# Three layers in one kernel: the latent layer's weights are loaded and folded earlier, and the expert layer's set-up moves into its main block

## The chip, the cores and the metric

The kernel runs on one core of one Trainium2 chip. TensorE (PE) multiplies matrices, VectorE (DVE), ScalarE (ACT) and GpSimd (POOL) do elementwise work, SyncE (SP) issues most DMAs. The metric is the device time of one execution in microseconds (us), as the median of several runs; lower is better.

## The reference

`x` has 8 batches of 512 tokens with 256 channels, in f32. Six steps follow each other, each on a layernorm of x:

```
x = x + 0.5 * L0_ffn(layernorm(x))     # 8 experts, gate's top 1; all experts are summed
x = x + L0_attn(layernorm(x))          # attention among the 16 heads of a token
x = x + 0.5 * L0_ffn(layernorm(x))
x = x + 0.5 * L1_ffn(layernorm(x))     # routed: 63 chosen tokens of a batch
x = x + L1_attn(layernorm(x))          # latent attention
x = x + 0.5 * L1_ffn(layernorm(x))
```

The routed layer weighs each token with one column, takes the best 63 of each batch, runs rope attention with an attention mask, gathered by row, and a gelu MLP over them, and puts them back. `position_ids` gives the angle of each token. The latent layer has 16 heads of 64, and a latent of 64:

```
q = x @ Wq;  c = x @ Wkv_down;  k = c @ Wk_up;  v = c @ Wv_up
out = softmax(causal(q @ k.T / 8)) @ v;  x = x + out @ Wout
```

## The kernel before, in words

`macaron_kernel` builds four layers one after the other: `expert_and_head_layers` (the first three steps), `routed_layer`, `latent_attention_layer`, `routed_layer` again. x stays in SBUF throughout. Each layer is a row of blocks.
**Expert layer.** A set-up block (L295 to L360) issues the load of batch 0 and of four weight chunks on SP, nine small loads on POOL, transposes three of the small tensors on TensorE and copies them on VectorE. In the main block SP loads the other weight chunks into four slots of `stage`; ScalarE writes their f16 high half (`split_chunk_head`), VectorE the low half (`split_chunk_tail`). Sixteen stages of 32 hidden tiles follow, each `up` and `down` in three f16 products, gelu on ScalarE, the low half of gelu on POOL (L760). The attention among heads runs on VectorE between them (`head_piece`). In the last stage VectorE does the router's statistics of seven batches ahead (`RouterEarly`).

**Routed layer.** The opening block (L1003 to L1119) loads the weights and the position rows (SP), makes index tiles (POOL), normalises x into `y` (32 operations on ScalarE, L1117) and picks the tokens: VectorE does the statistics of the last batch, waits for TensorE's transposes of `w_col` (L1099), then finds the best 64 in eight rounds (L1061, L1063), marks and numbers them (to L1088); TensorE transposes the marks (L1105). VectorE's list begins with a wait on the position rows' DMA and their cast (L1033). The main block starts with `one_hot` (L1508) and does attention and MLP.

**Latent layer.** The opening block (L1723 to L1827) loads the five weights, turns `Wk_up`, `Wv_up` and `Wq` on TensorE, and multiplies them head by head to `a` (Wq times Wk_up) and `b` (Wv_up times Wout): for each of 8 pairs of heads TensorE writes banks of PSUM (L1772, L1775), ScalarE writes the f16 high halves (L1825, L1826) and VectorE the low halves (L1813, L1815). POOL makes constants (L1735 to L1746), VectorE casts them and sets parts of the key, value and query tiles (L1782 to L1793). The main block is a pipeline over batches and heads (`stream`); its first operations are the layernorm statistics of batch 0 on VectorE, the variance on POOL, and the first guess of the root on VectorE (L49).

## Time and profile before

| | us |
|---|---|
| median of 3 runs | 2885.16 |
| lowest and highest run | 2885.03, 2890.66 |
| the profiled execution | 2883.19 |
| its span, first to last instruction | 2881.4 |

Busy time in that span: PE 2485.0 (86%), DVE 2123.2 (74%), ACT 1570.0 (54%), POOL 844.4 (29%). The page cuts the span in 40 slices of 72 us; a digit is the busy share in tenths, PEclk the granted clock of TensorE in tenths of 2.4 GHz:

```profile
PE   6999999989999999999999567688988888898376
PEclk9999999999999999999999666599999999999677
```

The expert layer fills the first 22 slices, the first routed layer is around slices 23 and 24, the latent layer follows to slice 37, and the second routed layer ends the row.

### The profile page before, as it was taken

The numbers are of one execution on the slowest core, as the hardware profiler recorded it, in microseconds if no ns is written. First come the engines' busy times: TensorE is split into PE (matmuls) and PEld (weight loads), VectorE is DVE, ScalarE is ACT, GpSimd is POOL, SyncE is SP. The second block draws the span as 40 slices with busy tenths as digits, with TensorE's granted clock in tenths as the row PEclk, the third lists the DMA queues.
The fourth block names the chain that finished last, engine by engine and source line by source line (L and its number), as shares of the span: only waits on it lengthen the run. The fifth ranks groups of instructions, "written<-read, shape, count | busy, mean of one in ns | idle before, by whom it ended". The sixth has DMA issues, their size and how long they took to land. (4 is left out here: it accounts for less than half of the span.)

```text
span 2881.4 us, 39763 instructions
## 1 busy us (share of the span) xinstructions
PE 2485.0 (86%) x14369; PEld 1352.2 (47%) x14369; DVE 2123.2 (74%) x3942; ACT 1570.0 (54%) x2517; POOL 844.4 (29%) x816
## 2 busy tenths in 40 slices
PE   6999999989999999999999567688988888898376
PEld 3444444444444444444444355255655555565254
DVE  3479688878979886888715654489788879877754
ACT  5655454555555554545554341277667767767251
POOL 3444333434443443434444100002112112202200
PEclk9999999999999999999999666599999999999677
DMA  5000000000000000000000101000000000000101
GB/s 167 28 1 1 0 1 1 1 1 1 1 1 1 1 1 1 1 1 1 1 1 1 63 1 38 1 1 2 2 2 3 2 3 2 2 2 2 49 16 59
DMA packets 29189, 33.11 MB, mean 11 GB/s; under 512 B 6408, under 2 KB 25416, under 8 KB 28984
## 3 DMA queue, kind: packets, MB, share of 16 engines
q1 hardware_dynamic: 28008, 27.89, 3.1%
q0 software_dynamic: 976, 2.56, 0.3%
q8 instruction: 120, 1.97, 0.3%
q14 instruction: 85, 0.70, 0.1%
HBM read 25.59 MB, written 4.19 MB: 10 GB/s over the span
## 5 line engine op out<-in xcount | busy, mean ns | idle before, releaser
L760 POOL TENSOR_TENSOR g_lo<-g_full,g_hi 128x512 f16<-128x512 f32 x512 | 659.0, 1290 | 910.1 <-ACT g_hi L851 908.1
L851 ACT ACTIVATE g_full<-hid,b_col 128x512 f32<-128x512 f32 x512 | 351.7, 687 | 559.5 <-PE hid L152 558.1
L150 PE MATMUL hid<-y_hi,w_hi 128*128 128x512 f16 x1024 | 396.0, 387 | 37.6 <-DVE y_lo L837 34.9
L151 PE MATMUL hid<-y_lo,w_hi 128*128 128x512 f16 x1024 | 395.2, 386 | 0.0
L152 PE MATMUL hid<-y_hi,w_lo 128*128 128x512 f16 x1024 | 394.7, 385 | 0.0
L150 PE MATMUL acc<-g_hi,w_hi 128*128 128x512 f16 x1024 | 388.9, 380 | 0.0
L151 PE MATMUL acc<-g_lo,w_hi 128*128 128x512 f16 x1024 | 388.9, 380 | 0.0
L152 PE MATMUL acc<-g_hi,w_lo 128*128 128x512 f16 x1024 | 388.6, 379 | 0.0
L851 ACT ACTIVATE g_hi<-hid,b_col 128x512 f16<-128x512 f32 x512 | 349.0, 682 | 0.0
L2095 DVE TENSOR_REDUCE mla_m_col<-mla_ps 128x1 f32<-128x512 f32 (+3 forms) x512 | 225.0, 483 | 62.3 <-PE mla_ps L1937 56.5
L2220 ACT ACTIVATE mla_p_full<-mla_ps 128x1280 f32<-128x1280 f32 x128 | 158.4, 1237 | 139.5 <-PE mla_ps L1967 139.2
L2195 DVE TENSOR_TENSOR mla_p_lo<-mla_p_full,mla_p_hi 128x1280 f16<-128x1280 f32 x128 | 205.5, 1605 | 3.2 <-ACT mla_p_hi L2220 2.6
L2257 POOL TENSOR_TENSOR mla_o_lo<-mla_o,mla_o_hi 128x512 f16<-128x512 f32 x64 | 107.2, 1680 | 326.6 <-ACT mla_o_hi L2229 326.6
L1936 PE MATMUL mla_ps<-mla_key_hl,mla_q_hi 128*128 128x512 f16 (+3 forms) x512 | 130.5, 308 | 69.3 <-DVE mla_m_col L2095 68.6
L721 DVE TENSOR_TENSOR prod<-score,v_rows 128x1024 f32<-128x1024 f32 x128 | 178.5, 1394 | 3.0
L150 PEld LDWEIGHTS hid<-y_hi,w_hi 128*128 128x128 f16 x1024 | 101.4, 99 | 161.7 <-DVE y_lo L837 38.9
L684 DVE TENSOR_TENSOR prod<-qk_rot 128x1024 f32<-128x1024 f32 x128 | 173.2, 1353 | 3.3
L1963 PE MATMUL mla_ps<-mla_q_hi,mla_key_hl 128*128 128x512 f16 (+3 forms) x512 | 156.3, 305 | 8.9 <-issue 6.4
L152 PEld LDWEIGHTS hid<-y_hi,w_lo 128*128 128x128 f16 x1024 | 101.8, 99 | 125.7 <-issue 8.6
L687 DVE TENSOR_REDUCE score<-prod 128x64 f32<-128x1024 f32 x128 | 156.2, 1220 | 4.4
L723 DVE TENSOR_REDUCE o_rows<-prod 128x64 f32<-128x1024 f32 x128 | 156.2, 1220 | 4.4
L2220 ACT ACTIVATE mla_p_hi<-mla_ps 128x1280 f16<-128x1280 f32 x128 | 157.6, 1231 | 0.0
(370 smaller groups left out, 4837.7 us busy)
## 6 DMA issues: line engine op xcount, KB each, us to landing
stage<-in_L_ffn_w_dram SPq DMA_DIRECT2D x16, 512.0 KB, 4.9
x<-in_L_attn_x_dram SPq DMA_DIRECT2D x8, 512.0 KB, 8.1
routed_w<-in_L_ffn_w_dram SPq DMA_DIRECT2D x4, 1024.0 KB, 8.1
out_dram<-x SPq DMA_DIRECT2D x8, 512.0 KB, 4.5
mla_sums<-mla_sum_row SPq DMA_DIRECT2D x128, 2.0 KB
mla_wq<-in_L_attn_Wq_dram SPq DMA_DIRECT2D x1, 1024.0 KB, 7.0
mla_wout<-in_L_attn_Wout_dram SPq DMA_DIRECT2D x1, 1024.0 KB, 9.2
routed_wqkv<-in_L_ffn_wq_dram SPq DMA_DIRECT2D x2, 256.0 KB, 2.9
```

The costliest lines, as they stand in the source:

```text
L150: pe.matmul(out, w_hi, v_hi, start=first, stop=False)
L151: pe.matmul(out, w_hi, v_lo, start=False, stop=False)
L152: return pe.matmul(out, w_lo, v_hi, start=False, stop=final)
L684: dve.tensor_tensor(pr, q4, k4, ALU.mult).then_inc(head_step, 1)
L687: dve.tensor_reduce(score[:, row:row + GROUP, :], pr, AX.X, ALU.add).then_inc(head_step, 1)
L721: dve.tensor_tensor(pr, e4, v4, ALU.mult).then_inc(head_step, 1)
L760: pool.tensor_tensor(g_lo[:, g, :], g_full[:, g, :], g_hi[:, g, :], ALU.subtract).then_inc(tail_done, 1)
L851: act.activation(out[:, g, :], hid[:, ht % 4, :], ACT.Gelu, bias=b1_col[:, ht:ht + 1], scale=1.0 / WS).then_inc(gelu_done, 1)
L1963: pe.matmul(flat[:, at:at + cols], key_hl[:, (slot + (h + 1) // H) % 2, toks], q_hi[:, hh % RING, t * P:], start=True, stop=False)
L2095: dve.tensor_reduce(m_col[:, g % 2, t, j:j + 1], flat[:, QUERY_AT[t]:QUERY_AT[t] + (t + 1) * P], AX.X, ALU.max).then_inc(s_max, 1)
L2195: dve.tensor_tensor(p_lo[:, hh % 2, :], p_full[:, hh % 2, :], p_hi[:, hh % 2, :], ALU.subtract).then_inc(p_tail, 1)
L2220: act.activation(out[:, hh % 2, :], flat[:, 3 * 512:3 * 512 + KEY_COLS], ACT.Exp, scale=float(MLA_DIM) ** -0.5).then_inc(exp_done, 1)
```

## The change

- The expert layer's set-up block is gone. Its loads, transposes (`small_turns`, into a bank of `acc`) and copies (`small_copies`) stand in the main block; TensorE and ScalarE wait for the five copies (`small_out`) before the first stage.
- `LatentSources`: `stage` becomes a tile that lasts into the first routed layer. Behind the last weight chunk SP waits for all chunk tails and loads the latent weights into it and into two smaller tiles.
- The position rows are loaded in the expert layer, cast once in its last stage and kept in `RouterEarly` for both routed layers.
- `LatentFold`: turns, folds and splits stand in the first routed layer's opening block. ScalarE copies from PSUM to f32 tiles, POOL makes both f16 halves. Six of the eight pairs stand on TensorE ahead of the pick's transposes, two behind. ScalarE's copies alternate with its normalisation from batch 2 on. POOL makes and casts the constants too. The second routed layer has no fold.
- The latent layer has no opening block. `set_tiles` holds the memsets, behind the statistics of batch 0; TensorE and SP wait for them.
- Tiles of the routed main block share memory (`sq` with `rot`, `p_t` with `mask_rows`, `o` and `o_t` with `mask_t`, `proc` with `s`), and its softmax waits for the last rotation.

```diff
+    def load(self, sp):
+        io = self.io
+        sp.dma_start(self.wk[:, :], io["Wk_up"].rearrange("c h n -> c (h n)")).then_inc(self.k_in, 16)
+        sp.dma_start(self.wv[:, :], io["Wv_up"].rearrange("c h n -> c (h n)")).then_inc(self.v_in, 16)
+        sp.dma_start(self.wq[:, :, :], io["Wq"].rearrange("(k p) h n -> p k (h n)", p=P)).then_inc(self.q_in, 16)
+        sp.dma_start(self.wout[:, :, :], io["Wout"].rearrange("(m h) n d -> (h n) m d", h=2)).then_inc(self.out_in, 16)
+        sp.dma_start(self.down[:, :, :], io["Wkv_down"].rearrange("(k p) c -> p k c", p=P)).then_inc(self.down_in, 16)
...
+        def small_turns(pe):
+            pe.wait_ge(small_in, 16 * SMALL_LOADS)
+            pe.wait_ge(ones_set, 1)
...
+            last.then_inc(small_t, 1)
+        def small_copies(dve):
+            dve.wait_ge(small_t, 1)
+            dve.tensor_copy(b1_col[:, :], small[:, 0:HID_TILES]).then_inc(small_out, 1)
...
+            dve.tensor_tensor(gate_lo[:, :, :], gate_t[:, :, :], gate_hi[:, :, :], ALU.subtract).then_inc(small_out, 1)
+        SMALL_STEPS = 5
...
+                small_turns(pe)
                 pe.wait_ge(normed, TILES)
                 transpose_tiles(pe, y, turn, ident[:, :]).then_inc(y_turned, 1)
+                pe.wait_ge(small_out, SMALL_STEPS)
...
+                small_copies(dve)
...
+                sp.dma_start(x[:, 0], io["x"][0].rearrange("(t p) d -> p t d", p=P)).then_inc(x_first, 16)
+                for c in range(SLOTS):
+                    load_chunk(sp, c)
...
+                sp.dma_start(early.pos_rows[:, :], io["position_ids"][:, 0:SEQ].rearrange("b (t p) -> b t p", p=P)
+                             ).then_inc(router_in, 16)
+                sp.wait_ge(chunk_tail, len(chunks))
+                sources.load(sp)
             @block.gpsimd
             def _(pool):
+                small_loads(pool)
...
+                act.wait_ge(small_out, SMALL_STEPS)
...
+    def turn(self, pe):
+        ps, first = self.ps, self.FIRST_BANK
+        for i, (w, there) in enumerate(((self.wk, self.k_in), (self.wv, self.v_in))):
+            pe.wait_ge(there, 16)
+            for m in range(MLA_PAIRS):
+                last = pe.transpose(ps[:, first + i, m * LATENT:(m + 1) * LATENT], w[:, m * P:(m + 1) * P],
+                                    self.ident[i * LATENT:(i + 1) * LATENT, i * LATENT:(i + 1) * LATENT])
+            last.then_inc(self.turned, 1)
+        pe.wait_ge(self.q_in, 16)
+        for m in range(MLA_PAIRS):
+            if m == 6:
+                pe.wait_ge(self.turn_out, 1)
+            bank = first + (2, 3, 4, 0)[m // 2]
+            for k in range(KD):
+                at = (m % 2) * D + k * P
+                last = pe.transpose(ps[:, bank, at:at + P], self.wq[:, k, m * P:(m + 1) * P], self.ident[:, :])
+            if m % 2 == 1:
+                last.then_inc(self.turned, 1)
+    def fold(self, pe, m):
+        if m == 0:
+            pe.wait_ge(self.out_in, 16)
+            pe.wait_ge(self.turn_out, 6)
+        if m >= 2:
+            pe.wait_ge(self.fold_out, m - 1)
+        for i in range(2):
+            bank = self.bank(m, i)
+            rows = slice(i * MLA_DIM, (i + 1) * MLA_DIM)
+            for k in range(KD):
+                pe.matmul(self.ps[:, bank, k * LATENT:(k + 1) * LATENT], self.wq_t[rows, m, k * P:(k + 1) * P],
+                          self.wk_t[rows, m, :], start=True, stop=True)
+            last = pe.matmul(self.ps[i * LATENT:(i + 1) * LATENT, bank, D:2 * D], self.wv_t[rows, m, :],
+                             self.wout[rows, m, :], start=True, stop=True)
+        last.then_inc(self.folded, 1)
+    def turned_copies(self, act):
...
+    def folded_copies(self, act, m):
+        act.wait_ge(self.folded, m + 1)
+        if m >= 2:
+            act.wait_ge(self.split_step, 4 * (m - 1))
+        for i in range(2):
+            rows = slice(i * LATENT, (i + 1) * LATENT)
+            act.activation(self.b_full[rows, m % 2, :], self.ps[rows, self.bank(m, i), D:2 * D], ACT.Copy, scale=WS)
+            last = act.activation(self.a_full[:, m % 2, :, i, :], self.folded_a(m, i), ACT.Copy, scale=WS)
+        last.then_inc(self.fold_out, 1)
+    def constants(self, pool):
+        to, made = self.to, self.made
...
+        for n, base in enumerate((0, -32)):
+            pool.wait_ge(made, 2 + n)
+            pool.affine_select(out=self.spread_f[:, :, :], in_=self.spread_f[:, :, :], compare_op=ALU.not_equal,
+                               fill=1.0 / INV_SCALE, base=base, pattern=[[-1, MLA_HEADS], [0, LATENT]],
+                               channel_multiplier=1).then_inc(made, 1)
...
+        pool.wait_ge(made, 6)
+        pool.tensor_copy(to.spread[:, :, :], self.spread_f[:, :, :])
+        pool.tensor_copy(to.block_q[:, :], self.block_f[:, 0, :])
+        pool.tensor_copy(to.block_k[:, :], self.block_f[:, 1, :])
+        pool.tensor_copy(to.ident_b[:, :], self.ident[:, :])
+        pool.wait_ge(self.down_in, 16)
+        pool.tensor_scalar(self.down[:, :, :], self.down[:, :, :], WS, None, ALU.mult).then_inc(self.down_step, 1)
+        pool.wait_ge(self.down_step, 1)
+        for i in range(2):
+            pool.tensor_copy(to.down_hi[:, :, i, :], self.down[:, :, :]).then_inc(self.down_step, 1)
+        pool.wait_ge(self.down_step, 3)
+        for i in range(2):
+            pool.tensor_tensor(to.down_lo[:, :, i, :], self.down[:, :, :], to.down_hi[:, :, i, :], ALU.subtract)
+    def split(self, pool, m):
+        to, slot = self.to, m % 2
+        a_hi, a_lo = (w[:, :, 2 * m:2 * m + 2, :] for w in (to.a_hi, to.a_lo))
+        pool.wait_ge(self.fold_out, m + 1)
+        pool.tensor_copy(a_hi, self.a_full[:, slot, :, :, :]).then_inc(self.split_step, 1)
+        pool.tensor_copy(to.b_hi[:, m, :], self.b_full[:, slot, :]).then_inc(self.split_step, 1)
+        pool.wait_ge(self.split_step, 4 * m + 2)
+        pool.tensor_tensor(a_lo, self.a_full[:, slot, :, :, :], a_hi, ALU.subtract).then_inc(self.split_step, 1)
+        pool.tensor_tensor(to.b_lo[:, m, :], self.b_full[:, slot, :], to.b_hi[:, m, :],
+                           ALU.subtract).then_inc(self.split_step, 1)
...
+                    if fold is not None:
+                        fold.constants(pool)
+                        for m in range(MLA_PAIRS):
+                            fold.split(pool, m)
-                    dve.wait_ge(small_in, 16)
-                    dve.tensor_copy(pos_rows_f[:, :], pos_rows[:, :]).then_inc(col_out, 1)
...
-                    pe.wait_ge(col_out, 1)
-                    pe.transpose(ps[:, 1, 0:16], pos_rows_f[:, :], ident[0:16, 0:16]).then_inc(cols_turned, 1)
+                    pe.transpose(ps[:, 1, 0:16], early.pos_rows_f[:, :], ident[0:16, 0:16]).then_inc(cols_turned, 1)
+                    if fold is not None:
+                        fold.turn(pe)
                     pe.wait_ge(weigh_step, TILES + 2)
                     for t in range(TILES):
                         last = pe.transpose(ps[0:BATCH, 0, t * P:(t + 1) * P], w_col[:, :, t], ident[:, :])
                     last.then_inc(rows_turned, 1)
+                    if fold is not None:
+                        for m in range(FOLDS_EARLY):
+                            fold.fold(pe, m)
                     pe.wait_ge(pick_step, 2 + 2 * (ROWS // 8) + 9)
                     for i, r in ((0, 5), (1, 3)):
                         for t in range(TILES):
                             last = pe.transpose(ps[:, 2, at:at + BATCH], row[:, r, t * P:(t + 1) * P],
                                                 ident[0:BATCH, 0:BATCH])
                     last.then_inc(cols_turned, 1)
+                    if fold is not None:
+                        for m in range(FOLDS_EARLY, MLA_PAIRS):
+                            fold.fold(pe, m)
                 @block.scalar
                 def _(act):
+                    if fold is not None:
+                        fold.turned_copies(act)
                     for b in range(BATCH):
                         if b == early.BATCHES:
                             act.wait_ge(norm_step, COLUMNS_AT)
+                        if fold is not None and b >= BATCH - FOLDS_EARLY:
+                            fold.folded_copies(act, b - BATCH + FOLDS_EARLY)
                         for t in range(TILES):
                             col = TILES * b + t
                             act.activation(y[:, b, t, 0:D], x[:, b, t, :], ACT.Identity, bias=shift[:, col:col + 1],
                                            scale=rstd[:, col:col + 1])
+                    if fold is not None:
+                        for m in range(FOLDS_EARLY, MLA_PAIRS):
+                            fold.folded_copies(act, m)
...
+                dve.wait_ge(rot_step, 8 * PAIRS)
...
+        def set_tiles(dve):
+            dve.memset(key_top[LATENT:P, :, :], 0.0).then_inc(zeroed, 1)
+            for slot in range(2):
+                dve.memset(val_hi[:, slot, :, LATENT:P], 1.0)
+                dve.memset(val_lo[:, slot, :, LATENT:P], 0.0)
+            dve.wait_ge(zeroed, 1)
+            dve.memset(key_top[LATENT:LATENT + 1, :, :], M_SCALE)
+            dve.memset(q_lo[LATENT:P, :, :], 0.0)
+            dve.memset(inv_hl[:, :], 0.0).then_inc(zeroed, 1)
...
+                if isinstance(b, int) and after == 0:
+                    set_tiles(dve)
...
+                pe.wait_ge(zeroed, 2)
```

## Rows read from the trace of the kernel before

**Rows 1.** Windows: stretch, length, busy of PE, PEld, DVE, ACT, POOL (count), PEclk, DMA, GB/s.

```profile
110.00:150.00 40.00, 40.00 (x196) 18.89 (x195) 15.29 (x54) 25.45 (x41) 15.89 (x14) 1.00 0.00 1
...
1585.00:1617.00 32.00, 2.32 (x13) 1.46 (x13) 25.34 (x74) 15.83 (x32) 1.88 (x12) 0.50 0.33 108
...
1762.00:1813.00 51.00, 39.22 (x128) 24.39 (x128) 20.23 (x53) 9.56 (x32) 4.17 (x12) 0.50 0.17 54
...
1790.00:1800.00 10.00, 10.00 (x30) 5.66 (x29) 3.33 (x11) 3.33 (x12) 0.00 (x0) 0.50 0.00 0
```

**Rows 2.** Timeline of the start: start us, us, engine, line, op [idle before].

```profile
13.22 0.31 PE L351 MATMUL small<-ident,b_rows 32*128 32x32 f32 x1 [13.22 <-DMA rope<-in_rope_tab_dram]
...
14.60 0.19 DVE L338 COPY b_col<-small 128x32 f32<-128x32 f32 x1 [14.60 <-PE small L358]
...
15.66 1.41 DVE L74 BATCH_NORM_STATS2 stats<-x 128x6 f32<-128x256 f32 x4 [0.30 <-PEq L314]
...
20.25 2.35 DVE L284 SCALAR_TENSOR_TENSOR w_lo<-stage,w_hi 128x1024 f16<-128x1024 f32 x2
...
24.50 1.29 DVE L646 CAST y_hi<-turn 128x512 f16<-128x512 f32 x2 [1.90 <-PE turn L144]
...
27.17 0.61 PE L150 MATMUL hid<-y_hi,w_hi 128*128 128x512 f16 x1 [2.71 <-DVE y_lo L649]
```

**Rows 3.** DMA issues of the first 16 us: KB each, us from issue to landing.

```profile
x<-in_L_attn_x_dram SPq DMA_DIRECT2D x1, 512.0 KB, 4.1
```

**Rows 4.** Timeline of the first routed layer's opening block, up to its main block.

```profile
1585.86 0.81 SPq L1006 DMA_DIRECT2D routed_pos_rows<-_L_ffn_position_ids_dram  x1
...
1588.31 0.21 DVE L1033 CAST routed_pos_rows_f<-routed_pos_rows 16x128 f32<-16x128 int32 x1 [4.86 <-DMA routed_pos_rows<-_L_ffn_position_ids_dram]
...
1595.42 1.02 PE L1099 MATMUL routed_ps<-ident,router_w_col 128*8 128x128 f32 x4 [6.55 <-DVE router_w_col L1043]
...
1615.82 1.02 PE L1105 MATMUL routed_ps<-ident,routed_row 8*128 8x8 f32 x8 [19.38 <-DVE routed_row L1088]
...
1617.42 1.81 POOL L1428 MEMSET routed_v_blk<- 128x2048 f32 x1 [29.66 <-POOLq L1003]
...
1617.46 2.77 DVE L1508 TENSOR_TENSOR routed_one_hot<-routed_iota_row,routed_slot_col 128x256 f32<-128x256 f32 x8 [0.30 <-PEq L1003]
```

**Rows 5.** Timeline of POOL and of DVE late in the expert stage, 1536 us.

```profile
1536.65 1.16 POOL L760 TENSOR_TENSOR g_lo<-g_full,g_hi 128x512 f16<-128x512 f32 x1 [1.43 <-ACT g_hi L851]
...
1536.71 1.13 DVE L57 TENSOR_TENSOR router_newton<-router_rstd 128x28 f32<-128x28 f32 x1
```

**Rows 6.** Timeline of the latent layer's opening block and first steps.

```profile
1762.69 0.26 POOL L1735 MEMSET mla_norm_const<- 128x4 f32 x6 [131.71 <-POOLq L2345]
...
1764.23 2.44 POOL L1740 TENSOR_SCALAR_AFFINE_SELECT mla_spread_f<-mla_spread_f 128x1024 f32<-128x1024 f32 x2
...
1768.29 0.27 DVE L1787 MEMSET mla_val_hi<- 128x256 f16 x1
...
1770.96 3.67 PE L1759 MATMUL mla_ps<-ident,mla_wq 128*128 128x128 f32 x16 [1.28 <-DMA mla_wq<-in_L_attn_Wq_dram]
...
1772.43 0.91 DVE L1793 MEMSET mla_key_top<- 1x1024 f16 x1 [0.27 <-DVE mla_key_top L1791]
...
1781.43 0.38 ACT L1825 ACTIVATE mla_b_hi<-mla_ps 64x256 f16<-64x256 f32 x1 [46.04 <-PE mla_ps L1775]
...
1782.37 0.28 ACT L1826 ACTIVATE mla_a_hi<-mla_ps 128x128 f16<-128x128 f32 x1
...
1813.48 1.41 DVE L74 BATCH_NORM_STATS2 mla_stats<-x 128x6 f32<-128x256 f32 x4 [0.32 <-PEq L1723]
...
1817.08 0.17 DVE L49 TENSOR_SCALAR mla_rstd<-mla_var 128x4 int32<-128x4 int32 x1 [2.20 <-POOL mla_minus_half L124]
```

**Rows 7.** One tile, mla_ps, in 1762:1813: min/median/max ns, first and last start.

```profile
L1775 PE MATMUL mla_ps<-mla_wout,mla_wv_t x32: 631/657/683, 1778.2 to 1809.9; 64*64 64x256 f32 x32
```

**Rows 8.** Timeline of DVE, the second routed layer's opening.

```profile
2700.66 0.21 DVE L1033 CAST routed_pos_rows_f<-routed_pos_rows 16x128 f32<-16x128 int32 x1 [6.02 <-DMA routed_pos_rows<-_L_ffn_position_ids_dram]
```

More of the change, by code:

```diff
@@ L152, in split_matmul, with __init__, sb, sem @@
     return pe.matmul(out, w_lo, v_hi, start=False, stop=final)
+BF16 = mybir.dt.bfloat16
+LATENT = 64
+MLA_HEADS, MLA_DIM = 16, 64
+MLA_PAIRS = MLA_HEADS // 2
+BLOCKED = -1.0e30
+M_SCALE, INV_SCALE = 64.0, 256.0
+GROUP_HEADS = 4
+LEAD = 8
+RING = LEAD
+SUM_SLOTS = 4
+SUM_ROWS = P // MLA_HEADS
+KEY_AT = (0, 512, 1024, 896)
+KEY_COLS = sum(SEQ - t * P for t in range(TILES))
+QUERY_AT = (512 + 384, 0, 512, 0)
+QUERY_TILES = (3, 2, 0, 1)
+PV_BANK = (7, 2)
+class LatentSources:
+    def __init__(self, nc, stack, program, io):
+        def sb(name, shape, dt=F32):
+            return stack.enter_context(nc.sbuf_tensor(f"latent_{name}", shape, dt, side="right"))
+        def sem(name):
+            return program.enter_context(nc.semaphore(f"latent_{name}"))
+        self.stack, self.io = stack, io
+        self.stage = sb("stage", [P, 4, 1024])
+        self.wq = self.stage[:, 0:KD, :]
+        self.wout = self.stage[:, KD:2 * KD, :].rearrange("p a n -> p (a n)").rearrange("p (m d) -> p m d", m=MLA_PAIRS)
+        kv = sb("kv", [P, MLA_HEADS * MLA_DIM])
+        self.wk, self.wv = kv[0:LATENT, :], kv[LATENT:P, :]
+        self.down = sb("down", [P, KD, LATENT])
+        self.k_in, self.v_in, self.q_in = sem("k_in"), sem("v_in"), sem("q_in")
+        self.out_in, self.down_in = sem("out_in"), sem("down_in")
+    def load(self, sp):
[5 more added lines that the diff above has]
+        sp.dma_start(self.down[:, :, :], io["Wkv_down"].rearrange("(k p) c -> p k c", p=P)).then_inc(self.down_in, 16)
 class RouterEarly:
@@ new lines, in small_turns @@
+        def small_turns(pe):
+            pe.wait_ge(small_in, 16 * SMALL_LOADS)
+            pe.wait_ge(ones_set, 1)
+            pe.transpose(small[:, 0:HID_TILES], b1_rows[:, :], ident[0:HID_TILES, 0:HID_TILES])
+            for k in range(KD):
+                pe.matmul(small[:, 64 + k:65 + k], b2_rows[:, k * P:(k + 1) * P], ones[:, :], start=True, stop=True)
+            for k in range(KD):
+                last = pe.transpose(small[:, 128 + k * EXPERTS:128 + (k + 1) * EXPERTS],
+                                    gate_rows[:, k * P:(k + 1) * P], ident[0:EXPERTS, 0:EXPERTS])
+            last.then_inc(small_t, 1)
@@ L944, in routed_layer @@
+def routed_layer(nc, keep, tag, x, ident, early, io, out=None, sources=None, latent=None):
     with ExitStack() as ctx:
@@ L996, in routed_layer @@
             cols_turned = tsem("cols_turned")
+            fold = LatentFold(nc, part, tsem, ps, ident, sources, latent) if latent is not None else None
+            if fold is not None:
+                part.push(sources.stack)
+            FOLDS_EARLY = MLA_PAIRS - 2
             COLUMNS_AT = TILES + LN_COLUMN_STEPS + 1
@@ L1118, in _ @@
                                            scale=rstd[:, col:col + 1])
+                    if fold is not None:
+                        for m in range(FOLDS_EARLY, MLA_PAIRS):
+                            fold.folded_copies(act, m)
         BLOCKS = HEADS // 4
@@ L2349, in _ @@
                             sp.sem_clear(semaphore)
-        layer(expert_and_head_layers, x, ident, early, experts)
-        layer(routed_layer, "routed1", x, ident, early, routed)
-        layer(latent_attention_layer, x, ident, early, latent)
+        with ExitStack() as lasting:
+            sources = LatentSources(nc, ExitStack(), ctx, latent)
+            layer(expert_and_head_layers, x, ident, early, sources, experts)
+            weights = LatentWeights(nc, lasting)
+            layer(routed_layer, "routed1", x, ident, early, routed, None, sources, weights)
+            layer(latent_attention_layer, x, ident, early, weights)
         layer(routed_layer, "routed2", x, ident, early, routed, out)
```

342 lines of the change are left out of this document (109 added, 233 removed).

## The prediction, made before the result was known

> **What bounds the kernel now.** I read the 40 slices of the page first. TensorE is at nine tenths in most slices of the expert stage, and there nothing but its own work counts (the window from 110 to 150 us: 40.00 of 40 us [rows 1]). The change touches none of that steady work, so I looked for the stretches where TensorE is not the bound and the blocks meet at barriers. The windows name two. The first routed layer's opening block (1585 to 1617) has 2.32 us of TensorE in 32 us and 25.34 us of VectorE: a serial chain on VectorE bounds it. The latent layer's opening block (1762 to 1813) has 39.22 us of TensorE at a granted clock of 0.50, the 1.2 GHz level, with no other engine above half: folding the weights on a slow TensorE bounds it. A third is the start, before the first `hid` matmul at 27.17 us [rows 2]. Then I read the timelines of each. Times below are counted from a block's first instruction where I say "at +x".
>
> **The start (set-up moved into the main block).** Before, the small loads land at 13.22, TensorE turns them, VectorE copies them at 14.60, then comes a barrier, and only then does VectorE start the layernorm of batch 0, at 15.66. Its chain runs to 20.25, where the two weight tails begin [rows 2]. The first batch had been there for long: x lands 4.1 us after its issue [rows 3], about 6 us. After the change the layernorm runs at 6 to 10.7 us (20.25 - 15.66 = 4.6 us of chain), under the wait for the small loads. ScalarE's halves of the first two chunks and the four applications also fit before 14.6. What is late next is the small loads: 13.22, TensorE done at 14.60, eight transposes (22.50 to 24.50 before, so 2.0) to 16.6. Beside them VectorE copies (0.8 us) to 15.4, then the tails (2.35) to 17.8, then four halves of y (24.50 to 27.17: 2.67) to 20.5. The first `hid` matmul starts there: 27.17 - 20.5 = **6.7 us gained**. All of it reaches the end, for TensorE is full afterwards. Bounds: 4 (if weight chunks or ScalarE come later than x) to 7.5.
>
> The latent loads (2.6 MB) and the position rows go to SP's queue behind the last chunk; SP has nothing later there, and nobody waits. The added cast of the position rows lies in VectorE's idle time. Both cost nothing.
>
> **Position rows.** The first routed block starts at 1585.86 and VectorE's chain only at 1588.45, after a cast that waited for a DMA [rows 4]. That goes: 2.6 us in each routed layer. In the first it enters the block sum below. In the second [rows 8] nothing else changes, so **2.6 us gained** (0 to 3).
>
> **The latent layer's opening block goes.** It runs from 1762.69 to VectorE's first statistics at 1813.48 [rows 6]: **50.8 us gained**. Given back: the memsets of the key, value and query tiles now stand on VectorE between the statistics and the root's first guess. Before, they ran from 1768.29 to 1773.34 (start of the last plus 0.91), 5.05 us with a 0.5 us gap; I take 4.8. The guess came 3.60 us after the statistics began (1817.08 - 1813.48); now it comes at 1.45 + 4.8 = 6.25: **2.65 us lost** (2.2 to 5, the upper end if VectorE and POOL get in each other's way).
>
> **The first routed layer's opening block grows.** Everything the fold needs is added to it, and it ends when the slowest of four engines ends. Step by step:
>
> - TensorE's 32 turns. Sixteen took 3.67 us [rows 6]; the smaller sixteen take at most as much. They end between +4 and +7.6.
> - VectorE's chain: w_col was ready at 1595.42, or +9.56; less 2.6 that is +7.0. But POOL now works beside it. A POOL subtraction of 1.16 us begins at 1536.65 and a VectorE operation of 28 columns, begun 0.06 us later, lasts 1.13 us, up to the same moment [rows 5]. Eight `one_hot` operations run beside a POOL memset in 2.77 us, 0.35 us each, unhindered [rows 4]. So POOL operations that read SBUF block VectorE's two-input ones. Here POOL reads from about +3.4: two selects of 1.22 us each [rows 6], two smaller, the casts, the split of `down`, about 7 us in all, across VectorE's 16 last small operations. I charge 3.0 us (0, if they slip between, to 5): w_col at +10.0.
> - TensorE turns w_col (1.02 us): +11.05. Then six pair folds. Sixteen half folds spanned 1777.2 to 1810.5, so 2.08 us each, 4.16 us a pair [rows 7]; the last matmul's 0.66 us is added to its start. Six take 25.0: +36.0. ScalarE (four copies, 1.22 us, and one batch of four applications at 15.83/32 = 0.49 us each [rows 1]: 3.2 us a pair) and POOL (below) are both faster than 4.16, so TensorE sets this pace.
> - The pick on VectorE takes 1596.44 to 1615.82, 19.4 us. It would be ready at +30.5, but its eight transposes stand behind the sixth fold in TensorE's order and start at +36.0. They end at +37.0.
> - The last two folds: 8.3 us, +45.35. ScalarE copies the last, 1.25: +46.6. POOL splits it: four operations of 256 columns. Rows 5 have 512 columns in 1.16 us; with the fixed part I take 0.68 for a subtraction and 0.5 for a cast, 2.4 us with the waits: +49.0. The barrier: +49.3.
>
> Before, the main block began at 1617.42, +31.56 [rows 4]. So **17.7 us lost**. ScalarE's applications, 15.83 us alone, end well before this. Bounds: +8 if the fold ran at the fast clock throughout, +22 if POOL is slow and the blocking is full.
>
> **Two rules of the Trainium skill.** "SBUF — State Buffer", section "Who interferes with whom", says that VectorE and GpSimd hold a shared port pair exclusively, and that a VectorE operation with two SBUF inputs blocks only against a GpSimd operation that reads. Rows 5 and the memset of rows 4 agree; without that rule the sum would be 3.0 us better. "TensorE: Matmul & The Clock Gate", section "The HAM clock gate", says that sustained activity releases the clock. Rows 1 do not show it for this fold: TensorE is busy 10.00 of 10 us and stays at 0.50. By the rule the fold would take half as long; that is the first rival.
>
> **The sum.** -6.7 - 2.6 - 50.8 + 2.65 + 17.7 = -39.75 us. The profiled execution took 2883.19 us (span 2881.4), 1.97 under the median of 2885.16; against the median I forecast 2845 us. The aliased tiles of the routed main block and its added wait on `rot_step` cost nothing: VectorE has done those rotations itself, in order, just before.
>
> **The rivals.**
>
> 1. The fold runs at 2.4 GHz (12%). For it: 6 us of unbroken transposes now precede it. Against it: rows 1. Then ScalarE's 3.2 us a pair sets the pace; six pairs end inside the pick, at about +29. The pick's transposes end at +31.5, two folds take 4.2, copies and split 3.7: +39.6, a loss of 8 instead of 17.7. Time: 2835.
> 2. The start gains nothing (8%): the first chunks or ScalarE's queue, which now holds a wait on five small copies ahead of the first Gelu, set the first `hid` matmul at 26 or later. Time: 2851.
> 3. POOL takes over the first routed opening (6%, of which half below the turning point). Casts and strided halves on POOL stand in no row. POOL can start its first split at +16.5 and has eight. At 1.5 us an operation (6 us a pair) it ends at +64.5: 15 us more, 2860. It is slower than before when the block's loss passes 17.7 + 39.75 = 57.5, an end at +89: (89 - 16.5)/8 = 9.1 us a pair, 2.3 us an operation, 3.5 times what rows 5 give. At 3 us an operation (12 us a pair) it ends at +112.5, a loss of 81, and the time is 2908.
> 4. The change doesn't do what it says (1%): the main block of the latent layer still waits for weights. Nothing there waits on the loads, and they have 1500 us.
>
> **How the numbers follow.** Forecast 73%, rivals 12, 8, 6 and 1%. Bounds of the unknown terms around 2845: -10 and -3 below, +5 (start 4 instead of 6.7, blocking, memsets) to +8 above; with rivals 1 and 2 inside, the range is 2833 to 2856. Faster by over 0.2% (5.8 us, about what a measurement of this kernel can tell from no change): 96%; within it 1%; slower 3%, the far half of rival 3.
>
> **What would show it.** The first `hid` matmul at 20.5 us. In the first routed opening: TensorE busy for some 45 us at clock 0.50, six folds 4.16 us apart, the pick's transposes waiting behind the sixth fold though VectorE has long been done, VectorE operations of over 1 us among the small ones, and the main block's first operation 49 us after the block's start. The latent layer: statistics within 0.5 us of the barrier, the guess 6.2 us later. The second routed layer: statistics at once. I am wrong if the fold's pairs come 3.2 us apart, if POOL is still splitting when ScalarE is long done, or if the first `hid` matmul stays near 27.

## The result, and the profile after

The changed kernel takes 2854.91 us (median of 4 runs, 2854.22 to 2856.62), against 2885.3 for the kernel before (median of 4 runs now, with one more than in the table above): a ratio of 0.9896, 95% interval 0.9884 to 0.9907. So 30.4 us were gained where I had forecast 40. The time is 9.9 us above the forecast and 1.1 us below the upper end of the range.

| | before | after |
|---|---|---|
| profiled execution, us | 2883.19 | 2856.62 |
| its span, us | 2881.4 | 2854.4 |
| TensorE busy, us | 2485.0 | 2490.6 |
| mean granted clock | 0.931 | 0.935 |

The page of the changed kernel (slices of 71 us; section 5: busy, mean ns | idle before, releaser) already names the surprise in the last two lines shown here (`g_lo` is the low half of the gelu's result, POOL's only work in this layer):

```profile
PE   7999999989999999999999777588888888898376
PEclk9999999999999999999999678699999999999677
...
L757 POOL TENSOR_TENSOR g_lo<-g_full,g_hi 128x512 f16<-128x512 f32 x512 | 670.5, 1313 | 900.6 <-ACT g_hi L849 899.0
...
L150 PE MATMUL acc<-g_hi,w_hi 128*128 128x512 f16 x1024 | 389.5, 380 | 5.2 <-POOL g_lo L757 5.2
```

The `acc` matmuls waited 5.2 us for `g_lo`, in one piece, in an expert layer that the change was not to touch.

I cut both spans at the same landmarks: the first `hid` matmul, the transposes after the last expert stage, the first POOL instruction of the routed opening, the first `one_hot`, the latent layer's first statistics, its first matmul, and the same in the second routed layer. Each length is the difference of two starts in the timelines, in us (from the last transposes to the routed opening it is 5.2 in both):

| stretch | before | after | difference | forecast |
|---|---|---|---|---|
| up to the first `hid` matmul | 27.17 | 20.05 | -7.1 | -6.7 |
| expert stages, to the last transposes | 1553.5 | 1562.7 | **+9.2** | 0 |
| first routed opening | 31.6 | 50.1 | +18.5 | +17.7 |
| its main part, up to the latent statistics (before, with the latent opening) | 196.0 | 145.7 | -50.3 | -50.8 |
| latent statistics to first matmul | 8.8 | 11.8 | +3.0 | +2.65 |
| rest of the latent layer | 875.6 | 878.4 | +2.8 | 0 |
| second routed opening | 31.9 | 29.0 | -2.9 | -2.6 |
| its main part, to the end | 151.6 | 151.35 | -0.25 | 0 |

The differences add up to -27.0, which is that of the spans (before rounding, -26.95). Five terms came out within 0.9 us. Two that I had at zero did not. The medians differ by 30.4 us, the spans of these two profiled executions by 27.0. That of the changed kernel is the slowest of its four, so some 3 us in the column of differences may be scatter of single executions.

**The start** (timeline, to be read beside [rows 2]): the small loads are turned as they land, the eight transposes of y follow at once, and the first `hid` matmul comes at 20.05.

```profile
13.03 0.31 PE L895 MATMUL acc<-ident,b_rows 32*128 32x32 f32 x1 [13.03 <-DMA rope<-in_rope_tab_dram]
...
14.29 1.97 PE L144 MATMUL turn<-ident,y 128*128 128x128 f32 x8
...
15.07 2.35 DVE L338 SCALAR_TENSOR_TENSOR w_lo<-latent_stage,w_hi 128x1024 f16<-128x1024 f32 x2
17.34 1.28 DVE L643 CAST y_hi<-turn 128x512 f16<-128x512 f32 x2
...
20.05 0.59 PE L150 MATMUL hid<-y_hi,w_hi 128*128 128x512 f16 x1 [3.79 <-DVE y_lo L646]
```

**The last expert stage.** First POOL, then VectorE, then TensorE, from three timelines of the same 20 us:

```profile
1533.44 1.18 POOL L757 TENSOR_TENSOR g_lo<-g_full,g_hi 128x512 f16<-128x512 f32 x1 [1.43 <-ACT g_hi L849]
1536.03 14.83 POOL L757 TENSOR_TENSOR g_lo<-g_full,g_hi 128x512 f16<-128x512 f32 x4 [1.41 <-ACT g_hi L849]
```

```profile
1534.92 0.21 DVE L789 CAST router_pos_rows_f<-router_pos_rows 16x128 f32<-16x128 int32 x1
1535.06 0.47 DVE L246 SCALAR_TENSOR_TENSOR rot<-x,router_ln_col,router_router 128x256 f32<-128x256 f32 x1
...
1535.87 0.47 DVE L246 SCALAR_TENSOR_TENSOR rot<-x,router_ln_col,router_router 128x256 f32<-128x256 f32 x1
...
1536.28 0.47 DVE L246 SCALAR_TENSOR_TENSOR rot<-x,router_ln_col,router_router 128x256 f32<-128x256 f32 x1
...
1546.04 0.47 DVE L246 SCALAR_TENSOR_TENSOR rot<-x,router_ln_col,router_router 128x256 f32<-128x256 f32 x1
```

```profile
1542.04 0.38 PE L152 MATMUL hid<-y_hi,w_lo 128*128 128x512 f16 x1
1547.58 0.61 PE L150 MATMUL acc<-g_hi,w_hi 128*128 128x512 f16 x1 [5.16 <-POOL g_lo L757]
...
1552.67 0.42 PE L150 MATMUL acc<-g_hi,w_hi 128*128 128x512 f16 x1
```

VectorE weighs 28 tiles for the router, each with two inputs in SBUF, 0.41 us from start to start and no gap. POOL's subtraction begins at 1536.03, within the third of them, and gets through only when all 28 are over: it takes 11.49 us by the tile's statistics (the 14.83 shown are four subtractions merged), where 1.16 is usual. I call this starving. The four buffers of `g` run dry, TensorE stands 5.16 us, and its next twelve matmuls are at the 1.2 GHz level, 5.09 us for what takes 12 x 0.216 = 2.6 at the other level (they were 0.216 us apart before). Together 5.16 + 2.5 = 7.7 us. In the kernel before the same 28 instructions let POOL in every 2.6 us. Its first arrival is 0.29 us into one of them, the next 0.36 us, and each time VectorE's following instruction is the one that waits (VectorE, then POOL, from the trace of before):

```profile
1541.54 0.48 DVE L192 SCALAR_TENSOR_TENSOR rot<-x,router_ln_col,router_router 128x256 f32<-128x256 f32 x1
1541.95 1.37 DVE L192 SCALAR_TENSOR_TENSOR rot<-x,router_ln_col,router_router 128x256 f32<-128x256 f32 x1
...
1544.06 0.47 DVE L192 SCALAR_TENSOR_TENSOR rot<-x,router_ln_col,router_router 128x256 f32<-128x256 f32 x1
```

```profile
1541.83 1.21 POOL L760 TENSOR_TENSOR g_lo<-g_full,g_hi 128x512 f16<-128x512 f32 x1 [1.41 <-ACT g_hi L851]
1544.42 1.15 POOL L760 TENSOR_TENSOR g_lo<-g_full,g_hi 128x512 f16<-128x512 f32 x1 [1.38 <-ACT g_hi L851]
```

One new instruction stands ahead of the weighing: the cast of the position rows, which makes it start 0.14 us later against POOL's rhythm.

**The routed opening** (timeline, to be read beside [rows 4]):

```profile
1587.97 1.41 DVE L232 BATCH_NORM_STATS2 router_stats<-x 128x6 f32<-128x256 f32 x4 [2.46 <-PEq L2404]
...
1589.76 1.39 DVE L85 TENSOR_SCALAR router_ln_col<-router_ln_col 128x4 f32<-128x4 f32 x1
1589.84 1.32 DVE L86 TENSOR_TENSOR router_ln_col<-router_ln_col 128x4 f32<-128x4 f32 x1
1589.94 0.94 POOL L1103 MEMSET fold_spread_f<- 128x1024 f32 x1
...
1599.05 1.02 PE L1300 MATMUL routed_ps<-ident,router_w_col 128*8 128x128 f32 x4 [5.69 <-DVE router_w_col L1243]
1600.00 1.11 PE L1073 MATMUL routed_ps<-fold_wk_t,fold_wq_t 64*128 64x64 f32 x4
...
1619.56 0.88 DVE L1288 TENSOR_SCALAR routed_row<-routed_w_row,routed_best 8x512 f32<-8x512 f32 x1
...
1624.96 1.02 PE L1309 MATMUL routed_ps<-ident,routed_row 8*128 8x8 f32 x8
...
1637.07 0.67 POOL L1136 TENSOR_TENSOR mla_b_lo<-fold_b_full,mla_b_hi 128x256 f16<-128x256 f32 x1
1638.05 1.80 POOL L1642 MEMSET routed_v_blk<- 128x2048 f32 x1 [0.31 <-SPq L1639]
```

TensorE has the weights column at +11.1 (forecast +10.0) and folds six pairs in 24.96 us (25.0). The pick's transposes stand behind the sixth fold though VectorE had finished 4.5 us earlier, and the main part starts at +50.1 (+49.3). VectorE's first long small operations (L85, L86) stand beside POOL's memsets, which read nothing; POOL's first select comes at 1591.28. A window (columns as in [rows 1]) shows a full TensorE at the slow level:

```profile
1600.00:1630.00 30.00, 30.00 (x93) 17.80 (x92) 19.76 (x37) 18.93 (x48) 14.37 (x24) 0.50 0.00 1
```

**The latent layer and the second routed layer** (timelines; [rows 6, 8]): the statistics start with the block, the memsets stand ahead of the guess, and the second pick starts at once (VectorE's first statistics at 2674.05, 0.02 us behind POOL's first instruction).

```profile
1783.81 1.41 DVE L74 BATCH_NORM_STATS2 mla_stats<-x 128x6 f32<-128x256 f32 x4 [3.75 <-PEq L2404]
1785.38 0.48 DVE L2144 MEMSET mla_key_top<- 64x512 uint32 x1 [0.16 <-issue]
...
1790.40 0.10 DVE L49 TENSOR_SCALAR mla_rstd<-mla_var 128x4 int32<-128x4 int32 x1
...
1795.61 1.09 PE L2060 MATMUL mla_ps<-ident,mla_y 128*128 128x128 f32 x4 [18.90 <-DVE mla_y L102]
...
2674.03 0.19 POOL L1217 IOTA routed_iota_row<- 128x64 f32 x1 [15.37 <-POOLq L2404]
...
2703.05 2.77 DVE L1722 TENSOR_TENSOR routed_one_hot<-routed_iota_row,routed_slot_col 128x256 f32<-128x256 f32 x8 [0.30 <-PEq L1203]
```

### The profile page after: what moved, and what is told of

The parts are those of the page before. It is cut to its first block and busy times, and to the rows that moved or that the text cites. A ratio compares the mean times of both kernels' runs of the same rounds, so it can differ in the third digit from the quotient of the medians.

```text
span 2854.4 us, 39741 instructions
## 1 busy us (share of the span) xinstructions
PE 2490.6 (87%) x14369; PEld 1354.2 (47%) x14369; DVE 2105.5 (74%) x3896; ACT 1573.0 (55%) x2523; POOL 877.8 (31%) x857
## 5 line engine op out<-in xcount | busy, mean ns | idle before, releaser
L757 POOL TENSOR_TENSOR g_lo<-g_full,g_hi 128x512 f16<-128x512 f32 x512 | 670.5, 1313 | 900.6 <-ACT g_hi L849 899.0
L150 PEld LDWEIGHTS acc<-g_hi,w_hi 128*128 128x128 f16 x1024 | 100.6, 98 | 127.3 <-POOL g_lo L757 5.9
```

Source lines behind the costliest of these rows:

```text
L150: pe.matmul(out, w_hi, v_hi, start=first, stop=False)
L757: pool.tensor_tensor(g_lo[:, g, :], g_full[:, g, :], g_hi[:, g, :], ALU.subtract).then_inc(tail_done, 1)
```

## Experiments on the lost 8 us

**1. The cast behind the weighing, not ahead of it.**

```diff
                 dve.wait_ge(router_in, 48)
-                dve.tensor_copy(early.pos_rows_f[:, :], early.pos_rows[:, :])
...
                     early.weigh(dve, early_step, early.COLUMNS_AT, x, TILES * (ht - EARLY_WEIGHTS_AT) + t, rot, 4)
+                if ht == EARLY_WEIGHTS_AT + early.BATCHES - 1:
+                    dve.tensor_copy(early.pos_rows_f[:, :], early.pos_rows[:, :])
```

> The changed kernel (2854.9 us) with one move: the copy of the position rows to f32 comes behind the 28 weighing instructions of the last expert stage, not ahead of them. Theory A: the 7.8 us lost in that stage come from one POOL subtraction (g_lo) that arrived 0.16 us into one of 28 back-to-back weighing instructions of DVE and was kept out until they ended; in the kernel before it arrived 0.29 us into one and was let in. The copy holds the weighing back by 0.14 us. Without it the arrival is at 0.30 us again: POOL's subtraction takes 1.2 us each time, no 5.2 us wait of TensorE on g_lo, time 2847. Theory B: the loss comes with another part of the change (earlier start, latent loads) and the copy has no share: the wait stays, time 2855.

Measured: 2847.2 us (2846.05 to 2850.65), ratio to before 0.987 (0.9853 to 0.9886). The longest `g_lo` of the stage is 1.20 us and the wait is gone. VectorE, then POOL, as they meet:

```profile
1535.44 0.48 DVE L246 SCALAR_TENSOR_TENSOR rot<-x,router_ln_col,router_router 128x256 f32<-128x256 f32 x1
1535.85 1.37 DVE L246 SCALAR_TENSOR_TENSOR rot<-x,router_ln_col,router_router 128x256 f32<-128x256 f32 x1
```

```profile
1535.74 1.20 POOL L757 TENSOR_TENSOR g_lo<-g_full,g_hi 128x512 f16<-128x512 f32 x1 [1.41 <-ACT g_hi L850]
```

POOL arrives 0.30 us into a weighing instruction, and it is VectorE's next one that waits (1.37 us). Moving one instruction of 0.2 us behind the 28 is worth 7.7 us.

**2. Gaps between the weighing instructions.**

```diff
-                    early.weigh(dve, early_step, early.COLUMNS_AT, x, TILES * (ht - EARLY_WEIGHTS_AT) + t, rot, 4)
+                    early.weigh(dve, early_step, early.COLUMNS_AT, x, TILES * (ht - EARLY_WEIGHTS_AT) + t, rot, 1)
```

> The changed kernel with one number changed: each weighing instruction of the last expert stage waits for the one before it (one scratch slot in place of four), so a gap opens between any two. Theory A (POOL is kept out only while DVE's instructions follow without a gap): the subtraction gets in at the next gap whatever its phase, at most 1.7 us for one, TensorE doesn't wait, 2847. Theory B (the loss has another source, or POOL is starved by the pair of engines whatever the gaps): 2855, the wait of 5.2 us stays.

Measured: 2845.98 us (2843.93 to 2849.01), 0.9862 (0.9845 to 0.9879). The instructions are 0.53 us apart instead of 0.41, POOL's longest takes 1.45 us, and TensorE never waits. The cast is still ahead of them. The first arrival, at 1536.33, happens to fall into a gap, but three later ones fall 0.05 us into an instruction, next to the 0.03 that is starved in experiment 5, and there POOL waits 0.3 us and gets in at the next gap (VectorE, then POOL):

```profile
1538.87 0.48 DVE L246 SCALAR_TENSOR_TENSOR rot<-x,router_ln_col,router_router 128x256 f32<-128x256 f32 x1
```

```profile
1538.92 1.44 POOL L757 TENSOR_TENSOR g_lo<-g_full,g_hi 128x512 f16<-128x512 f32 x1 [1.44 <-ACT g_hi L849]
```

**3. The kernel before, with only the cast added.**

```diff
+        self.pos_rows = stack.enter_context(nc.sbuf_tensor("router_pos_rows", [16, P], I32))
+        self.pos_rows_f = sb("pos_rows_f", [16, P])
...
-                dve.wait_ge(router_in, 32)
+                dve.wait_ge(router_in, 48)
+                dve.tensor_copy(early.pos_rows_f[:, :], early.pos_rows[:, :])
...
+                sp.dma_start(early.pos_rows[:, :], io["position_ids"][:, 0:SEQ].rearrange("b (t p) -> b t p", p=P)
+                             ).then_inc(router_in, 16)
```

> The kernel before (2885.3 us) with only the early load of the position rows and their copy to f32 ahead of the weighing; the routed opening still loads and converts its own. Theory A (the 0.14 us of the copy alone shift the weighing into the bad phase): one g_lo of some 11 to 15 us in the last expert stage, TensorE waits about 5 us and goes at half clock for about 5 us more, 2893. Theory B (another part of the change): 2885.

Measured: 2892.73 us (10 runs, 2889.38 to 2897.26), 1.0025 (1.0016 to 1.0035): slower by 7.7 us. The copy reproduces the loss in the kernel before, with none of the change's large parts:

```profile
1542.80 0.47 DVE L194 SCALAR_TENSOR_TENSOR rot<-x,router_ln_col,router_router 128x256 f32<-128x256 f32 x1
```

```profile
1542.96 11.49 POOL L762 TENSOR_TENSOR g_lo<-g_full,g_hi 128x512 f16<-128x512 f32 x1 [1.41 <-ACT g_hi L854]
```

The arrival is again 0.16 us into an instruction, and the duration again 11.49 us.

**4. The kernel before, with only the set-up moved** (`small_loads`, `small_turns` and `small_copies` as in the change's diff, without cast and latent loads).

> The kernel before with only the expert set-up moved into the main block. Theory A: the start's 7.1 us reach the end, since nothing stands ahead of the weighing that did not stand there before, 2878. Theory B (an earlier start is given back in the last expert stage): 2885, with a long g_lo there.

Measured: 2879.89 us (10 runs, 2876.11 to 2884.26), 0.9979 (0.997 to 0.9989), 5.1 us faster than the runs of before beside it (2885.02); the interval is 3.2 to 8.7 us. No `g_lo` is long (1.20 at most), and the first `hid` matmul is at 19.93. The interval holds the whole 7.2 us of the earlier start. By the landmarks its expert stages take 1554.6 us where those of the kernel before took 1553.5; in experiments 1 and 2 they took 1554.8 and 1554.6, and in experiment 3, with the old start, 1562.2, which less 7.7 is 1554.5. So the profile of before is the odd one, and the timelines show most of that microsecond in one place. After a pause of 2.6 us ahead of the transposes near 270 us, the next matmuls are 0.43 us apart, the 1.2 GHz level, in every one of these kernels (four or five of them, seven in experiment 3) and 0.216 us apart in the profile of before. The granted clock of the 15 us around is 1.00 before (272 to 287 us) and 0.89 in the changed kernel (264.5 to 279.5). Why it fell in one and not in the other is not shown. The latent layer took 878.4 us where that of before took 875.6, on which more below.

**5 and 6. Two copies, three copies.** Extra copies into a tile of their own shift the weighing by 0.14 us each.

```diff
                 dve.tensor_copy(early.pos_rows_f[:, :], early.pos_rows[:, :])
+                dve.tensor_copy(early.more_rows_f[:, 0, :], early.pos_rows[:, :])
+                dve.tensor_copy(early.more_rows_f[:, 1, :], early.pos_rows[:, :])   # the third, in 6 alone
```

> The changed kernel with a second copy of the position rows, into a tile of its own, behind the first: the weighing starts another 0.14 us later, and POOL's subtraction arrives 0.02 us into an instruction of DVE, not 0.16. Theory A (it is the place within one instruction that decides; arrivals at 0.00 to 0.07 and 0.29 to 0.37 were let in, those at 0.16 not): no long g_lo, 2847. Theory B (any copy, or any later start of the weighing, brings POOL's starving): a g_lo of over 10 us, 2855.

> The same with three copies: the arrival moves to 0.28 us into an instruction (of 0.41). Theory A: let in, as at 0.29, no long g_lo, 2847. Theory B: a g_lo of over 10 us, 2855.

Measured: 2854.43 us (2853.23 to 2857.07) with two, 2847.82 (one run) with three. VectorE and POOL with two copies, then with three:

```profile
1537.12 0.47 DVE L247 SCALAR_TENSOR_TENSOR rot<-x,router_ln_col,router_router 128x256 f32<-128x256 f32 x1
```

```profile
1537.15 13.84 POOL L758 TENSOR_TENSOR g_lo<-g_full,g_hi 128x512 f16<-128x512 f32 x3 [1.42 <-ACT g_hi L851]
```

```profile
1536.81 0.47 DVE L247 SCALAR_TENSOR_TENSOR rot<-x,router_ln_col,router_router 128x256 f32<-128x256 f32 x1
1537.21 1.37 DVE L247 SCALAR_TENSOR_TENSOR rot<-x,router_ln_col,router_router 128x256 f32<-128x256 f32 x1
```

```profile
1537.10 1.21 POOL L758 TENSOR_TENSOR g_lo<-g_full,g_hi 128x512 f16<-128x512 f32 x1 [1.41 <-ACT g_hi L852]
```

With two copies my forecast was wrong: an arrival 0.03 us in is starved too. I had read arrivals at 0.00 to 0.07 in the kernel before as let in, but there VectorE's instruction was the one that waited (1.44 us), so I take it that POOL had been first. With three the arrival is 0.29 us in, and the loss is gone, though the weighing starts later than ever. So neither the copy nor a later start is the cause; the place of the arrival within one instruction is. The first arrivals of all seven rows without gaps agree: 0.03, 0.16 and 0.16 starved; 0.29, 0.29, 0.29 and 0.30 let in, and in these four rows the second arrival, at 0.36, is let in as well.

## Experiments on the opening block and the latent start

All four have experiment 2's gaps, so they compare with its 2846.0 us and its opening of 50.1. They were measured in another set of runs, beside which the kernel before took 2887.1 us and not 2885.0; of the total the ratios to before are the better guide (0.9862 for experiment 2), and each has an interval of 0.003 or more.

**7. One fold ahead of the column's transposes.**

```diff
                         fold.turn(pe)
+                        fold.fold(pe, 0)
...
-                        for m in range(FOLDS_EARLY):
+                        for m in range(1, FOLDS_EARLY):
```

> The kernel with gaps between the weighing instructions (2846.0 us, opening of the first routed layer 50.1 us) and one more edit: the first of the six early pairs is folded ahead of the transposes of the weights column, where TensorE stood idle for some 5 us until DVE had the column. Theory A (the opening lasts as long as TensorE's chain of turns and eight folds at 4.16 us a pair, and the idle stretch ahead of it): one fold fits into the idle stretch, opening 45.9, time 2842. Theory B (DVE's picking sets the end, the folds lie beside it): the column comes no sooner, opening 50.1, 2846.

Measured: opening 45.96 us, time 2843.4 (2842.47 to 2846.45), ratio 0.9851. The length is as expected; of the 4.2 us the ratio shows 3.2, and its interval alone is too wide to prove them.

**8. The pick's transposes ahead of the sixth fold.**

```diff
-            FOLDS_EARLY = MLA_PAIRS - 2
+            FOLDS_EARLY = MLA_PAIRS - 3
```

> The kernel with gaps (2846.0 us) and the pick's transposes put ahead of the sixth fold (five early folds, not six): they no longer wait 4.5 us behind it. Theory A (TensorE's chain of folds is the bound): the slots come 4 us sooner, the last fold no sooner, opening 50.1, 2846. Theory B (the pick is late because of the sixth fold, and main waits for it): opening 45.9, 2842.

Measured: opening 50.12, 2847.4 us, ratio 0.9863. The transposes (PE L1309) start at +32.8 instead of +37.0, and the opening is no shorter. The wait behind the sixth fold, which I had listed in the chain, costs nothing by itself: TensorE's list is the bound, in whatever order.

**9. POOL's constants behind the weights column.**

```diff
+                        pool.wait_ge(weigh_step, TILES + 2)
                         fold.constants(pool)
```

> The kernel with gaps (2846.0 us), with POOL's building of the latent constants behind DVE's weights column, so that none of it lies beside DVE's column work. Theory A (POOL's selects and casts hold DVE's instructions back, some of 0.2 us take 1.0 to 1.4): the column is ready some 1.5 us sooner and all folds with it, opening 48.6, 2844.5. Theory B (DVE's chain takes its time anyway, the difference to the kernel before is chance): opening 50.1, 2846.

Measured: opening 46.04, 2845.25 us (2842.72 to 2847.55), ratio 0.9856. My expectation was right in kind and too small in size: the column is ready at +7.0, not +9.6. VectorE's small operation that took 1.32 us beside POOL's work takes 0.16 here, and TensorE has the column four microseconds sooner:

```profile
1582.61 0.16 DVE L86 TENSOR_TENSOR router_ln_col<-router_ln_col 128x4 f32<-128x4 f32 x1
```

```profile
1580.72 0.19 POOL L1217 IOTA routed_iota_row<- 128x64 f32 x1 [9.24 <-POOLq L2405]
```

```profile
1587.73 1.02 PE L1301 MATMUL routed_ps<-ident,router_w_col 128*8 128x128 f32 x4 [1.59 <-DVE router_w_col L1244]
```

**10. The tiles set behind the guess.** The call of `set_tiles` moves behind `rsqrt_start`.

> The kernel with gaps (2846.0 us), with the latent layer's zero and one tiles set behind the first guess of the inverse root, while POOL does its twelve Newton instructions (DVE idle 3.4 us), not ahead of it. Theory A: their 5.0 us mostly fit there; from the statistics to the first matmul 11.8 us become 10.5 to 8.8 (what does not fit in 3.4 us stays), time 2843.5 to 2845. Theory B (DVE's memsets keep POOL's small instructions out as the weighing did): 12 or more, 2846 or above.

Measured: 10.5 us from the statistics to the first matmul instead of 11.8, the upper end of what was expected, and POOL's small instructions undisturbed at 0.20 us. The time is 2849.05 (2844.26 to 2850.88), ratio 0.9862, the same as without the move: the first routed layer's main part, whose code is that of the others, took 147.8 us.

**11. All four edits, and 12. all but the tiles' move.**

> A version that joins four edits to the changed kernel (2854.9 us): gaps between the weighing instructions, one fold ahead of the column's transposes, POOL's constants behind the weights column, the tiles set behind the guess. Theory: the stretches add up as measured one by one, 8 us from the weighing, the opening block at 45.1 us in place of 50.1 (with the column at 7.0 us and a fold ahead of it TensorE has no gap left but its start, so the two opening edits give 5.0 together, not 8.2), 11.8 to 10.5 in the latent layer's start: 2840. Rival (the two opening edits add up): opening 42, 2837.

> The version with four edits without the move of the tiles in the latent layer (three edits left: gaps, one fold first, constants late). The version with four took 2843.1 us, 3 more than its stretches added up to, because the first routed layer's main part, whose code is the same in all, took 147.8 us, as in the other kernel with the tiles moved, against 144.0 to 145.7 in the rest. Theory A (which clock TensorE is granted there depends on where in time that part falls, chance of the build): any of 144 to 148 us; with 144.8 the time is 2842. Theory B (the move of the tiles makes the part ahead of it slower): 144.0 to 145.7, time 2841 to 2843; 147.8 refutes it. The opening is 45.2 us by both.

Measured: 2843.07 us (2842.55 to 2843.52), ratio 0.9854 (0.9837 to 0.987), opening 45.2, main part 147.8; and 2842.23 us (5 runs, 2840.94 to 2845.38), ratio 0.9846 (0.9833 to 0.986), opening 45.2, main part 145.6. The two opening edits give 5 us together, since TensorE's list is then full. The main part took 147.8 us in both kernels that have the tiles' move, and 144.0 to 145.7 in the nine others without a latent opening block. The granted clock makes the difference: the first 88 us of that part are alike in busy time in experiments 11 and 12, and of the next three stretches of 7.4 us the first and the third have 0.50 and 0.68 in experiment 11, 0.73 and 0.91 in experiment 12. Whether the move brings that about or chance did so twice stays open. Chance is large enough: the same code in the second routed layer took 151.2 to 154.2 us, and there the kernel with all four edits was the faster of the two (151.5 against 154.0). The version with three edits beats both kernels: 44 us under the one before, measured beside it, and 12.7 under the changed one, whose ratio (0.9884 to 0.9907) lies clear of its own.

## Why the forecast was right, and where it was not

- **"The added cast of the position rows lies in VectorE's idle time" and costs nothing: this step failed.** The cast itself is 0.21 us in an idle engine. It moves 28 two-input instructions by 0.14 us against POOL's rhythm, and POOL is starved for 10 us. Experiments 1 and 3 put its price at 7.7 us in either kernel. The sentence "All of it reaches the end" stands beside that: experiment 4 has the start alone, and its interval holds the whole gain. But in the total of the changed kernel the cast took back more than the start's 7.1 us.
- That the time is inside the range is in part luck. The upper margin of 8 us was made of a late start, more blocking and slow memsets. Of these some 1.5 us came (1.1 of blocking, 0.35 of memsets); what filled the rest was a loss that had no term.
- The start: -7.1 for -6.7, by the steps forecast (experiment 4 has it alone).
- The first routed opening: +18.5 for +17.7. The mis-sized term is POOL's blocking of VectorE, 4.1 us (column at +11.1, against +7.0 in experiment 9) where I charged 3.0. Its mechanism was told too narrowly. I let only POOL's reads block, and only two-input instructions of VectorE, from +3.4 on; but L85, an operation with one input, took 1.39 us from +1.8 on, beside POOL's memsets (0.17 in experiment 9), so about 1.2 of the 4.1 us came ahead of POOL's first read. Folds, pace, clock, tail and POOL's splits (0.40 a cast, 0.67 a subtraction; forecast 0.5 and 0.68) were right.
- The latent opening (-50.3 for -50.8), the tiles (+3.0 for +2.65) and the second pick (-2.9 for -2.6): right.
- The rest of the latent layer, +2.8, belongs to no step. The same instructions give 875.6, 878.4 and 882.0 us in one execution each of the kernel before and of experiments 4 and 3, none of which changes this layer; that of experiment 3 is the slowest of ten, which span 7.9 us. The eleven kernels with the change have 874.8 to 878.4. These windows (before, experiment 3) have the same 5584 matmuls with 740 and 746 us of busy time, 5.1 of the 6.4 us. For the same instructions I put that down to the granted clock falling in different places; the rest is idle time.

```profile
1813.48:2697.86 884.38, 740.49 (x5584) 475.58 (x5584) 716.27 (x1295) 573.51 (x722) 156.65 (x241) 0.95 0.01 2
```

```profile
1821.43:2712.19 890.76, 745.56 (x5584) 477.98 (x5584) 716.73 (x1295) 573.65 (x721) 157.03 (x240) 0.95 0.01 2
```

- Rival 1 (fold at the fast level): no, 30.00 of 30 us busy at 0.50. Rival 2 (start gains nothing): no. Rival 3 (POOL takes over): no; its last split ended 2.2 us after ScalarE's last copy. Rival 4: no, the latent main part waited for no weights.

I had seen the blocking in [rows 5] and used it in one direction only: POOL holds, VectorE waits. The same rows raise the question for the other direction, and the place to ask it was the longest unbroken run of two-input VectorE instructions beside POOL's `g_lo`, where I was adding an instruction.

The Trainium skill ("SBUF — State Buffer", section "Who interferes with whom") calls the port pair that VectorE and GpSimd share an exclusive lock, and says of VectorE's 2-port modes that whoever issues first has it for the whole instruction while the other blocks. Carried over to a two-input instruction, the traces agree on who waits, and differ on how long: POOL, once too late, was not served at the end of that one instruction, nor of the next 24 (11.49 us where the rule would give 1.16 + 0.25). That it is the ports, and not something else that the two engines share, is argued and not shown: no run weighs with only one input in SBUF. What the runs show is the row, the gap and the place of the arrival.

## What to carry to other kernels

Ask of every long run of back-to-back VectorE instructions with two SBUF inputs what a POOL instruction that arrives in the middle would do, and what buffer runs dry meanwhile; a gap after each (here 0.12 us) removes this chance at no cost when VectorE has time. An instruction that costs nothing can still shift one engine's rhythm against another's, so look for what it stands ahead of. And where one engine's list is the bound of a block, fill its first idle stretch before reordering its end.

## What the runs showed of the hardware

- Starving is decided by 0.1 us. In a row of VectorE instructions 0.41 us apart, a POOL subtraction that arrived 0.03 or 0.16 us into one waited to the end of the row (11.49 us in all for 0.16), one that arrived at 0.29, 0.30 or 0.36 got in behind it. What lies between 0.16 and 0.29 was not tried. With 0.12 us between the instructions an arrival at 0.05 waited 0.3 us only.
- Small VectorE operations, also one with a single input, took 0.9 to 1.4 us beside POOL's memsets, selects and casts, and 0.16 or 0.17 without them.
- A 5.2 us idle stretch of TensorE in the expert layer was followed by 5.1 us at the 1.2 GHz level: the idle time cost half as much again.
- The same instructions of the latent layer took 874.8 to 882.0 us in the profiled executions of fourteen kernels; between 875.6 and 882.0, 5.1 of the 6.4 us are busy time of the same matmuls, which only the granted clock is known to change here. A gain of 2 or 3 us in a kernel of this kind is seen in the length of its stretch, not in the total.
